# Two transformer layers in one kernel: transfers timed one by one in the written orders, keys, values and queries loaded apart, and other buffers for the rows of layer two

## The reference, cut to what matters

```python
x = x + attn0(layernorm(x), ctx)   # kv = ctx @ W_k.T + b; out = p @ kv; softmax(layernorm(out @ kv.T) * gamma + beta)
x = x + ffn0(layernorm(x))         # rms(gelu(n@w_gate) * (n@w_up) @ w_down) + rms(mixture of 2 of 8 experts), rms of the sum
x = x + attn1(layernorm(x), ctx)   # 16 query heads, 4 key heads of 32, rms norms, rotary, causal softmax, @ w_out.T
x = x + ffn1(layernorm(x))         # silu(x@w_gate.T) * (x@w_up.T) @ w_down.T, hidden size 2048
```

## Time and profile before

| | |
|---|---|
| median of 3 runs | 2016.03 us (2008.18 to 2016.49) |
| profiled execution, its own time | 2012.14 us |
| span of that execution | 2010.4 us |
| PE busy | 1739.0 us (86%), 9396 matmuls |
| DVE busy | 1185.7 us (59%) |
| ACT busy | 806.0 us (40%) |
| POOL busy | 244.5 us (12%) |
| mean granted clock of PE | 0.940 of full speed |
| bytes moved | 409.52 MB, mean 204 GB/s |

### The profile page before, as it was taken

One profiled execution on the slowest core, in us unless ns is written; L12 is line 12 of the kernel. 1 busy time (PEld: TensorE's weight loads), 2 busy tenths in 40 slices (PEclk: granted clock), 3 DMA queues, 4 the chain that ended last, 5 costly groups with the idle time before them and its releaser, 6 DMA issues. The chain is left out here.

```text
span 2010.4 us, 27378 instructions
## 1 busy us (share of the span) xinstructions
PE 1739.0 (86%) x9396; PEld 1369.5 (68%) x9396; DVE 1185.7 (59%) x2583; ACT 806.0 (40%) x1804; POOL 244.5 (12%) x253
## 2 busy tenths in 40 slices
PE   4687897788988998887999899968899769999998
PEld 3566775566888886666767676756676446778887
DVE  6587774373656656877566566648775435553333
ACT  4364552232655653232444365432225435431111
POOL 1233315290000002221000000011310000000000
PEclk9697998998999999998999999989999879999999
DMA  3465459977667788666734553577777025235563
GB/s 102 151 220 204 158 163 347 338 291 277 231 238 274 261 312 329 215 257 224 237 90 123 197 168 117 178 294 267 290 251 231 1 54 156 64 126 201 197 211 104
DMA packets 135464, 409.52 MB, mean 204 GB/s; under 512 B 15136, under 2 KB 29856, under 8 KB 129568
## 3 DMA queue, kind: packets, MB, share of 16 engines
q1 hardware_dynamic: 125200, 372.65, 53.9%
q0 software_dynamic: 10128, 35.13, 4.6%
HBM read 282.95 MB, written 124.78 MB: 203 GB/s over the span
## 5 line engine op out<-in xcount | busy, mean ns | idle before, releaser
L1133 PE MATMUL ps<-xT,gu 128*128 128x512 f32 (+1 forms) x1392 | 538.8, 387 | 88.3 <-DVE act L1611 31.2
L1135 PE MATMUL ps<-xT,gu 128*128 128x512 f32 (+1 forms) x1392 | 515.6, 370 | 0.0
L1134 PE MATMUL ps<-xT,gu 128*128 128x512 f32 (+1 forms) x1392 | 514.7, 370 | 0.0
L1133 PEld LDWEIGHTS ps<-xT,gu 128*128 128x128 f32 x1392 | 271.6, 195 | 149.7 <-DVE act L1611 36.9
L1133 PE MATMUL ps<-wd,hid 128*128 128x512 f32 x604 | 252.6, 418 | 58.4 <-DVE acc L1646 31.8
L1135 PEld LDWEIGHTS ps<-xT,gu 128*128 128x128 f32 x1392 | 270.2, 194 | 44.6
L1134 PEld LDWEIGHTS ps<-xT,gu 128*128 128x128 f32 x1392 | 271.9, 195 | 36.2
L1134 PE MATMUL ps<-wd,hid 128*128 128x512 f32 x604 | 242.8, 402 | 0.0
L1135 PE MATMUL ps<-wd,hid 128*128 128x512 f32 x604 | 242.5, 402 | 0.0
L1338 ACT ACTIVATE hid<-act 128x512 fp32r<-128x512 f32 (+1 forms) x174 | 99.9, 574 | 296.8 <-DVE act L1611 296.6
L1626 DVE TENSOR_TENSOR gu<-raw,gu 128x512 fp32r<-128x512 f32 x188 | 134.7, 739 | 101.5 <-ACT gu L1354 101.0
(11 more groups left out here) (275 smaller groups left out, 2422.0 us busy)
## 6 DMA issues: line engine op xcount, KB each, us to landing
gu<-w_dram SPq DMA_DIRECT2D x160, 512.0 KB, 4.3
raw<-in_ffn_w SPq DMA_DIRECT2D x94, 768.0 KB, 5.6
wd<-w_dram SPq DMA_DIRECT2D x80, 512.0 KB, 5.3
w_dram<-gu SPq DMA_DIRECT2D x32, 1024.0 KB, 8.6
w_dram<-wd SPq DMA_DIRECT2D x32, 512.0 KB, 9.4
QT<-q_dram SPq DMA_DIRECT2D x48, 256.0 KB, 6.9
xg_dram<-zt POOLq DMA_DIRECT2D x23, 512.0 KB, 6.8
x<-xg_dram SPq DMA_DIRECT2D x23, 512.0 KB, 5.9
```

What stands on the lines that cost most here:

```text
L1133: mm(out_ap, ah, bh, start=start, stop=False)
L1134: mm(out_ap, ah, bl, start=False, stop=False)
L1135: return mm(out_ap, al, bh, start=False, stop=stop)
```

## The change

The order of MAIN becomes 0, 1, experts, 2, 3 for layer one; `x_slot` becomes 0, 1, 1, 0 for layer one's sequences 0 to 3 and 1 - b % 2 for layer two's. `xn4` gets a buffer of its own, in memory that `aTh` and `aTl` (the split attention result) also use; the first split of a sequence now waits for the turned rows of the sequence before, and the softmax no longer does.

In the orders, `bload` falls apart into `ktload`, `vload`, `woload` and four `qload` items, each with its own wait; `fetch` keeps POOL's gather alone, which now needs only `parts` of the sequence before, and SP gets `drows` (needs `final`) and `mrows` (needs the query row); the next context load, `cload`, `wostore` and POOL's `xsload` (the reading of rows to be scattered to the experts) become items too. The planner gets a table `MOVED` with the number of issues, size and extra latency of each transfer, a single shared transfer engine at 330 KB per us, 0.35 us of SP for each issue, and a model of PE's clock (`on_clock`). The fixed lags go.

```diff
-    TURN = (0, 1, 3, 2)
-    MAIN = [*dense(0, TURN[0]), *dense(0, TURN[1])[:SPLIT], *EXPERTS, *dense(0, TURN[1])[SPLIT:], *dense(0, TURN[2]), *dense(0, TURN[3]), *dense(1, 0), ...]
+    MAIN = [*dense(0, 0), *dense(0, 1), *EXPERTS, *dense(0, 2), *dense(0, 3), *(tile for b in range(B) for tile in dense(1, b))]
...
-        return b % 2
+        return 1 - b % 2 if f else (0, 1, 1, 0)[b]
...
+    MOVED = {"raw": (1, 768, 0), "pre": (1, 512, 0), "wstore": (2, 1536, 0), "xs": (1, 512, 0), ..., "kload": (7, 1792, 4), ..., "fetch": (0, 512, 4), ...}
...
-            "fetch": lambda: ([("mload", b - b % 2), ("dstore", LAST_DOWN["F", 0, b], TB - 1)] + [("qrow", b - 1, i), ("x2store", b - 1, i)] * (b % 2), 6 if b % 2 else 8),
+            "drows": lambda: [("mload", b - b % 2), ("dstore", LAST_DOWN["F", 0, b], i)] + [("final", b - 1, i)] * (b % 2),
+            "mrows": lambda: [("mload", b - b % 2), ("x1store", B - 1)] + [("qrow", b - 1, i), ("x2store", b - 1, i)] * (b % 2),
+            "fetch": lambda: [("mload", b - b % 2), ("dstore", *LAST_MOE[1:])] + [("parts", b - 1, i)] * (b % 2),
...
+        def on_clock(t, us):
...
+                        t = now[0] = on_clock(max(t, now[0]), us)
...
+                move = moves(item)
+                for engine, us in steps(item) + ([("SP", 0.35 * move[0])] if move and move[0] else []):
...
+                if move:
+                    _, size, extra = move
+                    start, n = reserve("DMA", kind, t, size / 330)
+                    busy["DMA"].insert(n, (start, start + size / 330, None))
+                    t = max(t + size / 270, start + size / 330) + 1.9 + extra
...
-        xn4 = Pr[:, 0, 0:2, :]
+        xn4 = sb("xn4", [P, 2, D], F32, b_scope)
...
-                elif kind == "bload":
+                elif kind == "ktload":
                     b = a[0]
                     if b % 2:
-                        sp.wait_ge(s_done, nth("scores", b - 1, NU - 1, HG - 1))
-                        sp.wait_ge(pv_done, nth("values", b - 1, NU - 1, TB - 1))
+                        sp.wait_ge(s_done, nth(*last_scores(b - 1, TB - 1)))
...
-                    load_queries(b, 0)
+                elif kind == "vload":
+                    b = a[0]
+                    if b % 2:
+                        sp.wait_ge(pv_done, nth("values", b - 1, NU - 1, TB - 1))
...
-                    if n == 0 and p == 0:
-                        act_.wait_ge(row4_turned, TB * b)
...
+                    if qt == 0:
+                        act_.wait_ge(row4_turned, TB * b)
                     func(aTh[:, :, :], aT[:, :, :], ACT.Copy).then_inc(attn_high, 1)
```

More of the change, by code:

```diff
@@ L297, in builds_on @@
                 on.append(("xgt", b, RB - 1) if what == "E" else ("rowt4", b, TB - 1) if f else ("xtload", b) if b else ("xt", 0, TB - 1))
-            return on, 14 if what == "F" and f == 0 and b and h == 0 else 0 if is_raw(a[0]) else 4
+            return on
         if kind in QUARTERS and kind != "up0":
[L300 to L304, removed]
@@ new lines, in builds_on @@
+            "xtload": lambda: [("xtstore", b, i) for i in range(TB)] + [x_free(b)] + [("xtload", b - 1)] * (b > 1),
+            "top2": lambda: [("logit", B - 1, TB - 1)], "ranks": lambda: [("top2", 2)], "weights": lambda: [("top2", 2)], "before": lambda: [("ranks",)], "blocks": lambda: [("before", 2)],
+            "places": lambda: [("blocks", 3), ("weights",)], "slots": lambda: [("places", 2)],
+            "scatter": lambda: [("slots", 1), ("zero", NB - 1), ("xsload", b)],
+            "xsload": lambda: [("scatter", b - 4)] if b > 3 else [("x1store", n) for n in range(B)] + [("xstore", B - 1, n) for n in range(TB)],
@@ L377, in merge @@
         end, holder, downs, placed = {}, {}, [1], []
-        busy = {"ACT": [], "DVE": [], "POOL": [], "SP": []}
+        busy = {"ACT": [], "DVE": [], "POOL": [], "SP": [], "DMA": []}
         tensor, now, last_of = [], [0.0], {}
         row_turns, row_norms = [], []
+        work, slow = {}, [1]
         def taken(item):
@@ L388, in ready @@
             for item in tick:
-                on, lag = builds_on(item)
-                on = [o for o in on if o not in inside and min(o[1:], default=0) >= 0]
+                on = [o for o in builds_on(item) if o not in inside and min(o[1:], default=0) >= 0]
                 if any(o not in end for o in on):
@@ L393, in ready @@
                 if not inside:
[L394 removed]
+                    at = max([end[o] for o in on], default=0.0)
                 if item[0] == "rowt" and row_norms[len(row_turns)] != item[1:]:
@@ L407, in ready @@
             return at
+        def on_clock(t, us):
+            while us > 1e-6:
+                n = int(t / WINDOW + 1e-9)
+                while len(slow) <= n:
+                    slow.append(2 if work.get(len(slow) - 1, 0.0) < (0.38 if slow[-1] == 1 else 0.65) * WINDOW else 1)
+                span = min((n + 1) * WINDOW - t, us * slow[n])
+                work[n] = work.get(n, 0.0) + span
+                us -= span / slow[n]
+                t += span
+            return t
         def on_tensor(tick):
@@ L426, in place @@
                 kind = "w" if item[0] == "wo" else item[0]
-                on, lag = builds_on(item)
-                t = max([end[o] + lag for o in on if o in end] + [at])
+                t = max([end[o] for o in builds_on(item) if o in end] + [at])
                 for n in taken(item):
```

205 lines of the change are left out of this document (107 added, 98 removed).

## The result

The changed kernel takes 1904.1 us (median of 4 runs, 1901.8 to 1907.3) beside 2014.3 us for the kernel before in the same measurement: ratio 0.9459, 95% interval 0.9431 to 0.9486. That is 110 us less, where 53 were forecast and 1923 was the low end of the range. The direction was right; the size was not.

A forecast was written before the change was run, and what follows sets the result against it. PE was taken to bound the kernel, with attention 2 running without dense tiles. Cover 40, part 1's 7 and part 3's 6 sum to 53 us: 2012.1 to 1959, or 1963 on the median's footing; range 1923 to 2014.

The forecast's parts named there:

- What bounds the kernel: Whole kernel: PE bounds it; at 1553.6 to 1652.4 us it lacks dense tiles, and SP's silence is not the cause.
- the lone stretch: 1553.6 to 1652.4 us: attention 2 runs without dense tiles, PE busy 66.2 of 98.8 us; its price is 43 us.
- Part 1: Sequence order, xT halves, own xn4: attention 1 starts 38 us earlier, gaining 7 us (0 to 11).
- Both together move the chain: Attention 2 starts 38 + 25 + 25 = 88 us earlier against the dense tiles; 45 suffice to cover it.
- the cover: Dense tiles beside the last 0.70 of attention 2: gains 40 of 43 us (bounds 0 and 43).
- Part 2: Mid stages: gathers 52 us earlier through separate transfers, 25 us taken for each stage (0 to 45), no gain by itself.
- the prediction's sign for rival A: If the mid stages keep their 204 and 212 us, part 2 is wrong and rival A holds.
- rival A: Attention 2: cover only partial, the lone stretch may keep half; gain 27 us, 1989 us; chance 0.17.
- Part 3: Planner's transfer table: 6 us (-8 to 24) from a DVE wait at 1323 to 1336; other reshuffling 0 (-20 to +20).
- The Trainium skill's rule: SP and GpSimd transfers interleave on the same 16 engines, so splitting them was given no gain in bandwidth.
- B: Mid stages: DVE waits for late dn with PSUM adds behind, 24 us each, three cases 72 us: 2035 us; chance 0.14.
- C: New order loses 20 us before 750 us and 16 in a mid stage, with A's gain: about 2014; chance 0.09.

The follow-up runs named there:

- one_load: Changed kernel with keys, first two queries, values and output weights as one SP item again, waiting for the last value product: 1896.4 us.
- old_lags: Changed kernel, its planner given back fixed lags, with no SP issue time, shared transfer engine or clock: 1976.3 us.
- late_gather: Changed kernel with an odd sequence's gathers and dense rows placed after the even one's query row again in the planner: 1904.8 us.
- b_table: Kernel before, only its planner's transfer lags replaced by size, latency and one shared transfer engine: 1955.6 us.
- share_only: Changed kernel with old_lags' fixed lags, no SP time and no clock, but transfers sharing one engine in the planner: 1911.7 us.
- store_blind: Changed kernel whose planner gives the weight stores no size, only issue and 1.9 us: 1918.5 us.
- old_struct: Changed kernel's table and items, with the old sequence order, xT halves, shared xn4 buffer and joined load: 1933.8 us.
- b_struct: Kernel before with only the new sequence order, xT halves and xn4's own buffer; old planner, loads and lags: 1998.2 us.
- late_xsload: Changed kernel, in whose planner the experts' rows are read only once the slots are known, as before: 1910.2 us.
- one_load_look: one_load with planner settings LOOK 0.5 for 1.0 and AHEAD 8 for 12: 1892.0 us.
- n_sp: Changed kernel with issues on SP taking no time in the planner, 0 for 0.35 us: 1900.0 us.

## Why the prediction was wrong, point by point

**What bounds the kernel: right.** PE bounds it, and the lone stretch was due to missing dense tiles and not to the silent SP queue: one_load still asks for the next keys only after the last value product, and its dense tiles reach over the whole of attention 2 (sequence 1's end at 1565 us, attention 2 at 1511).

**Part 1 and the chain: nearly right in the changed kernel, not without the new table.** The freed buffers moved attention 1 by 34 us (38 forecast). "Both together move the chain" added a shift at its head up to its end as if the stages between kept their length. On the old planner 11 of 34 us arrived. In the changed kernel attention 2 starts 699.7 us after the experts for 771.3: 72 us earlier, of 88, and 45 were enough for the cover. This step did not make the miss. The 40 us that it priced the cover at are another matter: old_lags has the cover and wins 17 us behind the experts.

**Part 2: right at the adds, wrong for the stages.** Its 25 us for each mid stage were 14 and 0. The gather came 51 us earlier against the add before it, as worked out, and the adds of sequence 1 followed those of sequence 0 by 25 us less (86.2 to 61.4), those of sequence 3 by 19 less (84.7 to 65.8). But from a stage's last add to its first scores it took longer, 85 us for 73 and 78 for 59; what holds it there was not found. DVE is busy 155.4 of 211.9 us in the first stage, and PE 175.1, so "DVE is the busiest thing in the mid stages" was misread from the earlier trace rows too (152.7 beside PE's 168.5). late_gather makes the first mid stage 23 us longer, the second 13 shorter and the kernel no slower: there was slack for it. The loads apart moved attention 1 forward by 11 us more, which brought no time either (one_load). The second mid stage kept its length, the prediction's sign for rival A, and the cover is whole all the same: that sign did not tell what it was to tell.

**Part 3: the failed step, and most of the miss.** It had 6 us for one DVE wait of 12.7, and for all the reshuffling "I have no row that gives it a sign: 0". Measured: 56 us on the old kernel with nothing else (b_table), 72 on the new (old_lags), 65 of them back by sharing alone (share_only). A row for it was there: the 58.4 us of idle PE before down triples, behind DVE's adds. b_table leaves 23.9 of them, 34.5 us less, though 14.5 come back before gate/up triples. I took one instance of a repeated wait for the whole of it. ACT's 44.2 us behind `w_dram<-gu` look like the same loss, but store_blind has them back at 45.0 us and loses 11 to 14, so stalls behind stores are a part and not the whole. Which waits make up the rest of the 72 was not taken apart. Before the end of the experts PE had 95.6 us idle; the changed kernel has 62.1, and 8.6 us less of busy time and a start 6.7 us earlier do the rest of 49.

The sum by stages: 49 us to the end of the experts (0 forecast), 61 us behind it (53 forecast). The second number looks like a hit and is luck in good part: with all of the structure and the old lags (old_lags) it is 17, and the table makes the other 44 of it. The table also covers much without part 1: the lone stretch is 39 us long in b_table and 28 in old_struct (1545 to 1573).

The Trainium skill's rule (DMA: Bandwidth & Descriptors, "Issuing engines are not separate DMA queues") was weighed against the split loads. one_load agrees in so far as the loads apart gain nothing, but those loads are all SP's own, and so are both landings that the prediction named, a load's and a store's: no run here tests SP's transfers against GpSimd's. By the same rule a planner with one shared transfer engine is the closer model, and I drew nothing from that: share_only against old_lags is its price, 65 us.

**Rivals.** A is out, the cover is whole. B is out: the idle time before down triples fell from 58.4 to 17.7 us. C is out, PE's idle time in the first 750 us fell from 144.3 to 115.4 us; its own sum was wrong besides, since 2016 - 27 + 36 is 2025 and not 2014. What was missing is a rival on the fast side.

**Open.** Some 20 us before the end of the experts are won with the items and the old kind of table (old_lags 721.1 and before 741.2; b_struct 743.5), but b_table gets 42 of the 49 with the old items, so the two overlap. Which of the smaller dependencies does it wasn't found; late_xsload excludes one. Why one_load is faster than the loads apart was not settled either; it may be the scatter between orders. Nor was why the mid stages lost again behind their adds what they had won ahead of them.

## What to carry to other kernels

Where orders are written ahead from a table of costs, a shared resource left out of the table can cost more than any one buffer: here 56 to 72 us beside 15 to 30 for the structure. A shift at the head of a chain is not a shift at its end: ask of each stage between what it will now overlap. When one instance of a wait is found, look for its total in the groups before giving it a price, and test that price by itself: a total of idle time is not yet time won.

## What the runs showed of the hardware

The 16 transfer engines can be kept busy nearly all of a long stretch: one_load_look runs layer one's dense tiles of sequence 1, with raw loads, kept stores and the scatter beside them, in 152.7 us (184.4 before, 162.7 in the changed kernel) at a DMA share of 0.97 and 364 GB/s (0.83 and 310, 0.89 and 335).

```profile
268.70:421.40 152.70, 139.15 (x609) 113.12 (x609) 86.12 (x196) 55.67 (x119) 61.11 (x86) 0.98 0.97 364
```

A single issue on SP is not always short. In the second mid stage of before a raw load takes 0.33 us of the queue and, 22 us later, another takes 3.05. Earlier, in a stretch with the transfer engines busy throughout, a load of 64 KB in rows of 128 bytes took 8.51; in the changed kernel the same load took 3.30. What makes them long was not tested:

```profile
1299.01 0.33 SPq L794 DMA_DIRECT2D raw<-in_ffn_w  x1
...
1321.41 3.05 SPq L794 DMA_DIRECT2D raw<-in_ffn_w  x1
```

```profile
383.90 8.51 SPq L917 DMA_DIRECT2D cosB<-in_cos  x1
```

Charging SP's issues in the planner at 0.35 us each or at nothing made no difference that can be seen (n_sp).
